# Moved waits, the value copy before the probability copy, and a new ending of the last phase, in a state-space plus local-attention kernel

## The reference

```python
for l in range(6):                                   # B=2, N=1024, D=128, 16 heads of 64
    q, k, v = split(x @ Wqkv[l])                     # 128 -> 3 x 1024
    q, k = rotary(l2norm(q) * qs, l2norm(k) * ks)
    p = softmax(8 * q @ k.T)                         # windows of 32 queries over 64 keys
    x = x + (p @ v) @ Wo[l]
    a, g = split(layernorm(x) @ W1[l] + b1)          # 128 -> 2 x 341
    x = x + (a * gelu(g)) @ W2[l] + b2
out = resid + gate * x
```

## Time and profile before

| | |
|---|---|
| time, median of 3 | 2083.33 us (2079.34 to 2084.64) |
| the profiled execution, its own time | 2082.23 us |
| its span, first to last instruction | 2080.4 us |
| PE busy | 1992.2 us (96%) |
| DVE busy | 1520.1 us (73%) |
| ACT busy | 1383.3 us (66%) |
| POOL busy | 1227.6 us (59%) |
| granted PE clock, mean | 0.975 of full speed |

### The profile page before, as it was taken

The page is one execution under the profiler, slowest core; times in us unless marked ns, Lnnn a source line. Parts: engine busy times, 40 slices in busy tenths (PEclk is TensorE's granted clock), DMA queues, the critical chain, the costliest instruction groups (busy, mean ns, idle before and its releaser), DMA issues. The chain is left out here.

```text
span 2080.4 us, 82225 instructions
## 1 busy us (share of the span) xinstructions
PE 1992.2 (96%) x32996; PEld 1395.7 (67%) x32996; DVE 1520.1 (73%) x2879; ACT 1383.3 (66%) x4165; POOL 1227.6 (59%) x1376
## 2 busy tenths in 40 slices
PE   7788798999999999999999999999999999999987
PEld 3333233887687786876877868768768677687672
DVE  1499896886786776867867768679678687686763
ACT  4532233886786776867867777678678776686772
POOL 1376774775585564855756756559456566575550
PEclk9888888999999999999999999999999999999998
DMA  1421110311131111221111211112211111121110
GB/s 62 134 71 71 60 61 4 102 44 39 38 93 40 38 44 32 50 84 37 47 36 40 87 37 45 38 35 57 79 38 47 38 41 40 32 54 30 27 29 21
DMA packets 148091, 104.30 MB, mean 50 GB/s; under 512 B 15778, under 2 KB 140256, under 8 KB 146176
## 3 DMA queue, kind: packets, MB, share of 16 engines
q1 hardware_dynamic: 147712, 99.07, 17.1%
HBM read 48.31 MB, written 1.18 MB: 24 GB/s over the span
## 5 line engine op out<-in xcount | busy, mean ns | idle before, releaser
L1401 POOL TENSOR_TENSOR QK<-QK,RN 128x512 f32<-128x512 f32 x384 | 400.2, 1042 | 375.2 <-ACT RN L1134 360.1
L1144 ACT ACTIVATE PR<-ps,MN 128x64 f32<-128x64 f32 x1536 | 355.9, 315 | 155.6 <-DVE MN L1262 140.0
L1009 PE MATMUL ps<-W,XS 128*128 128x256 f32 x1536 | 434.9, 406 | 5.1 <-PEq L64 4.1
L1396 POOL TENSOR_TENSOR QK<-PC,PS 128x256 f32<-128x256 f32 x384 | 279.7, 728 | 247.8 <-PE ps L995 243.8
L1170 ACT COPY QKT<-ps 128x512 f32<-128x512 f32 x384 | 224.6, 585 | 245.9 <-PE ps L995 245.8
L1286 DVE TENSOR_REDUCE SS<-SQ 128x8 f32<-128x512 f32 x384 | 262.2, 683 | 57.6 <-ACT SQ L1177 55.6
L1009 PEld LDWEIGHTS ps<-W,XS 128*128 128x128 f32 x1536 | 260.8, 189 | 61.6 <-issue 4.9
L1397 POOL TENSOR_TENSOR QK<-PC,PS 128x256 f32<-128x256 f32 x384 | 280.8, 731 | 0.0
L1262 DVE TENSOR_REDUCE MN<-ps 128x4 f32<-128x256 f32 x384 | 162.9, 424 | 149.8 <-PE ps L957 148.1
L1305 DVE TENSOR_TENSOR PC<-ps,TC 128x512 f32<-128x512 f32 x384 | 261.2, 680 | 0.1
L1307 DVE TENSOR_TENSOR PS<-ps,TS 128x512 f32<-128x512 f32 x384 | 260.4, 678 | 0.0
(11 more groups left out here) (137 smaller groups left out, 3216.3 us busy)
## 6 DMA issues: line engine op xcount, KB each, us to landing
V<-V SPq DMA_DIRECT2D x384, 97.5 KB, 2.2
scr<-B_rows SPq DMA_DIRECT2D x32, 512.0 KB, 3.6
V<-V SPq DMA_DIRECT2D x288, 32.5 KB, 2.4
W<-in_Wqkv SPq DMA_DIRECT2D x40, 192.0 KB, 2.9
TC<-in_tcos SPq DMA_DIRECT2D x6, 1024.0 KB, 5.1
TS<-in_tsin SPq DMA_DIRECT2D x6, 1024.0 KB, 8.5
WO<-in_Wo SPq DMA_DIRECT2D x6, 512.0 KB, 4.1
W<-in_W SPq DMA_DIRECT2D x6, 341.0 KB
```

Of the source, the lines that this page charges most:

```text
L1009: mm = nc.tensor.matmul(ps[:, par, k * 2 * P:(k + 1) * 2 * P], cols[k], W[:, i, 0:2, :].rearrange("p t m -> p (t m)"), start=True, stop=True)
L1144: e = nc.scalar.activation(PR[:, m % 2, h, slot * DH:(slot + 1) * DH], ps[:, 3 + h, slot * DH:(slot + 1) * DH], ACT.Exp, scale=-1.0, bias= ...
L1396: nc.gpsimd.tensor_tensor(QK[:, par, :, 0:hd], PC[:, par, :, 0:hd], PS[:, par, :, hd:DH], ALU.add)
L1401: nc.gpsimd.tensor_tensor(QK[:, par, :, :], QK[:, par, :, :], bcast_last(RN[:, m // 2 % 2, 8 * par:8 * par + 8], DH), ALU.mult).then_inc(q ...
```

## The change

There are four parts.

1. In steady steps the first value product loses its wait for `v_cp`, and the first projection product its wait for `prods`. The wait for `prods` goes to the first mask product. The wait for `pT` at the first score product stays.
2. ACT copies V before PT (in the feed-forward step too, between the GELUs).
3. Eight draining steps are left behind step 384. Ten of the sixteen output products of the last phase are issued inside them (`early_wo`), after the probability transposes of their step. The rest of the phase follows in code of its own, over six banks instead of one; DVE takes the layer norm's scaling from POOL.
4. The output is no longer formed by DVE and transposed. `out_rows` lets PE add `XRES.T` and `XT.T @ diag(gate)` in one bank, with two products of 128x128 for each 128 columns; POOL makes the two diagonal matrices DG at the start. Batch 0's rows are made in the ending before the feed-forward, batch 1's last.

```diff
@@ scores, values, project
+                    if steady(n) and h == 0:
+                        pe.wait_ge(prods, n - 1)
...
-                wait(pe, v_cp, min(n, NSTEPS))
+                    wait(pe, v_cp, min(n, NSTEPS))
...
-                wait(pe, prods, n - 1)
+                if not steady(n):
+                    wait(pe, prods, n - 1)
...
@@ places and banks
+        LAST = 2 * DEPTH - 1
+        DRAIN = NSTEPS + 8
+        early_wo = {1: [(0, 0), (0, 1)], 2: [(0, 2)], 3: [(0, 3)], 4: [(0, 4), (0, 5)], 5: [(0, 6)],
+                    6: [(0, 7), (1, 0), (1, 1)]}
...
+            return (7, 0, 3)[k % 3] if t == LAST else (2, 7)[k % 2]
...
@@ new functions on PE
+            def out_pair(t, c, k):
+                mm = nc.tensor.matmul(ps[:, wo_bank(t, c), :], WO[:, k, :], OT[:, c, k, :], start=(k == 0),
+                                      stop=(k == PAIRS - 1), skip_group_check=True)
...
+            def out_rows(b, c, bank):
+                for k in range(4):
+                    cols = slice((2 * b + c) * CH + k * P, (2 * b + c) * CH + (k + 1) * P)
+                    nc.tensor.matmul(ps[:, bank, k * P:(k + 1) * P], XRES[:, cols], ident[:], start=True, stop=False)
+                    mm = nc.tensor.matmul(ps[:, bank, k * P:(k + 1) * P], XT[:, cols], DG[:, b, :], start=False, stop=True)
...
+                if n == NSTEPS + 1:
+                    pe.wait_ge(prods, NSTEPS)
+                for c, k in early_wo.get(n - NSTEPS, ()):
+                    pe.wait_ge(oT, PHASE * LAST + 4 * k + 2 + 2 * c)
+                    out_pair(LAST, c, k)
...
@@ ACT
                     copy_out(n)
                     squares(n)
+                    copy_v(n)
                     copy_p(n)
-                    copy_v(n)
...
+            deviation(LAST, 0)
+            inverse(LAST, 0)
+            copy_rows(0)
+            copy_rows(1)
+            deviation(LAST, 1)
+            inverse(LAST, 1)
+            load_set(nc, act, GELU)
+            gates(LAST, range(6))
+            copy_rows(2)
+            copy_rows(3)
...
@@ DVE
+            for c in range(2):
+                add_attn(LAST, c)
+                centre(LAST, c)
+                dve.wait_ge(fsq, 2 * LAST + c + 1)
+                last_norm(c)
+            hidden(LAST)
+            add_ffn(LAST)
```

More of the change, by code:

```diff
@@ L864, in _ @@
             sp.wait_ge(s_v0, 1)
-            for n in range(NSTEPS + PHASE):
-                u, t = n % PHASE, n // PHASE - 1
+            for n in range(DRAIN):
+                u, t = n % PHASE, n // PHASE - 1 if n < NSTEPS else -1
                 if n < NSTEPS:
@@ L1081, in feed_forward @@
                         pe.wait_ge(hid, 6 * t + k - 1)
-                    nc.tensor.matmul(ps[0:size, banks[k % 2], :], W1[:, m0:m0 + size], CEN[:, c, :],
-                                     start=True, stop=True).then_inc(up_ps, 1)
+                    up_product(t, k)
                 if t % 2 == 0:
@@ L1087, in feed_forward @@
                     pe.wait_ge(hid, 6 * t + 5 + c)
[L1088 to L1094, removed]
+                    w2_product(t, c)
+            def out_rows(b, c, bank):
[3 more added lines that the diff above has]
+                    mm = nc.tensor.matmul(ps[:, bank, k * P:(k + 1) * P], XT[:, cols], DG[:, b, :], start=False, stop=True)
+                mm.then_inc(fT_ps, 1)
+            for n in range(DRAIN):
+                u, t = n % PHASE, n // PHASE - 1 if n < NSTEPS else -1
                 if u == U_FFN + 1 and t >= 0:
@@ L1218, in gates @@
                     wait(act, w2_ps, 2 * t)
-                    nc.scalar.activation(HID[0:size, c, m, :], ps[0:size, banks[k % 2], :], ACT.Gelu,
+                    nc.scalar.activation(HID[0:size, c, m, :], ps[0:size, gate_bank(t, k), :], ACT.Gelu,
                                          bias=vec(6 + m, t // 2, size)).then_inc(gel, 1)
-            for n in range(NSTEPS + PHASE):
-                u, t = n % PHASE, n // PHASE - 1
+            for n in range(DRAIN):
+                u, t = n % PHASE, n // PHASE - 1 if n < NSTEPS else -1
                 norm_pair(n)
@@ L1249, in _, with copy_rows @@
                             inverse(t, c)
[L1250 removed]
+            def copy_rows(c):
                 act.wait_ge(fT_ps, c + 1)
[L1252 removed]
+                nc.scalar.copy(OUT[:, 4 * c:4 * c + 4, :].rearrange("p k m -> p (k m)"), ps[:, 3 + c, :]).then_inc(fcp, 1)
+            deviation(LAST, 0)
[8 more added lines that the diff above has]
+            copy_rows(3)
         @block.vector
@@ L1374, in _ @@
             nc.gpsimd.memset(lnb[:], float(np.log(LN_SCALE) / 2)).then_inc(s_lnb, 1)
+            for b in range(B):
+                nc.gpsimd.tensor_scalar(DG[:, b, :], ident[:], MOD[:, 5, b:b + 1], None, ALU.mult).then_inc(s_dg, 1)
             def scale_rows(l):
```

162 lines of the change are left out of this document (110 added, 52 removed).

## The result

The changed kernel takes 2100.12 us (median of 3 runs, 2095.63 to 2100.2), against 2083.33 us. The ratio is 1.0078, with a 95% interval of 1.0048 to 1.0107: slower, by more than the bound that the prediction set for a case of its own (0.3%), where it had forecast 2080 us and held 2088 us for the upper end. The profiled execution took 2095.63 us, its span is 2093.8 us (2080.4 before).

The account below looks back on a forecast made before the run. PE was taken as busy throughout regular stretches, with ACT's ring of copies next at 0.01 us. +7.4 + 2.7 + 0 - 13.5 = -3.4 us gave 2079.9 us from 2083.33, forecast as 2080, range 2072.5 to 2088.

Parts of the forecast that it names:

- Part 1, the waits that go: Waits dropped at PE's first value and projection products: already over, the gap comes of the shape change, so worth 0.
- Part 2, V ahead of PT: ACT's copy order: PT still released 0.01 us ahead of the score load, so regular steps give 0 to -3 us.
- the eleven places: Places, one per phase, where PT is already last to come and its 0.26 us delay counts nearly in full: +2.7 us.
- rival C: V can't start before 1304.03, so PT is 0.03 to 0.04 us late every regular step: 2089 to 2092; chance 0.12.
- Part 1, the wait that is added: First mask product waits for `prods` behind POOL's table scalings: 20 of 40 places at 0.37 us, +7.4 us, at most +14.8.
- Parts 3 and 4, the ending: Output products moved into the drain and a reworked ending: saves 13.5 us, between 10 and 17.
- the walk: Piece-by-piece timing of the new ending, from chunk 0's projection done at 2028.7 to the end at 2066.6, saving 13.8.
- Four products enter this ring: In the drain, four output products at 0.89 us delay the chain of transposes, scores, values and DVE's ON: +3.5 us.
- about 2 us stick: Of the three output products behind those four in the drain, about 2 us remain as cost.
- A: Removed waits did cost something, ACT's ring gives its 0.01 us and the ending saves 16: -8.9 us, 2074.4; chance 0.30.
- the ring: ACT's chain from score products through exponents, squares and copies back to scores: leaves 0.01 us, at most -3 us in all.
- B: Every table scaling pays its 0.37 us at the mask, 14.8 in all: +4.0 us, 2087.3; chance 0.15.

Follow-up runs that it names:

- Run 3: The kernel before with V copied ahead of PT and the first value product's wait for `v_cp` removed in steady steps: 2111.76 us, ratio 1.0147.
- run 2: The kernel before with only the order of ACT's copies changed, V ahead of PT: 2107.56 us, ratio 1.0138.
- run 5: The kernel before with V copied ahead of PT, and SP also waiting for PT's copy before it issues V's two shifts: 2100.02 us, ratio 1.0076.
- run 4: The kernel before with only the wait for `prods` moved to the first mask product in steady steps: 2093.4 us, ratio 1.0052.
- run 7: The kernel before with the `prods` wait moved to the mask and DVE's clamp replaced by a bias in ACT's logarithm: 2084.3 us, ratio 0.9998.
- run 1: The changed kernel with parts 1 and 2 taken back, so the new ending alone: 2064.1 us, ratio 0.9917 to the kernel before.

## Why the prediction was wrong

**The sign.** It was made of -13.5 for the ending and +10.1 for the rest. In the profiled executions, cut at the last full step, these are -15.2 and +30.3; another -1.6 lies ahead of the first scores, a stretch that lasts 371.4 to 377.8 us in the kernels here though no edit is aimed at it. The gain came about nearly as forecast; the loss was three times the forecast one.

**Part 1, the waits that go: right.** Run 3 beside run 2 differs by 0.2 us in the steady part. The gap at the change of shape stayed: from the last value product's start to the projection's load are 0.145 us in the median before and after. The Trainium skill's rule that a change of the tiling mode empties the engine ("TensorEngine Tiling (Array Packing)", section Key Properties), which the prediction cites, spoke for the same, and the trace agrees with it by this 0.145.

**Part 2, V ahead of PT: the step that failed.** "PT 1304.25, its end 1304.62, release 1304.67. The load stands at 1304.68. So a regular step costs 0, with 0.01 us to spare." The start was right. The end was put together from two rows that don't go together: the earliest start, 0.49 us behind the squares, from the earlier trace rows, and the duration 0.37 from the earlier trace rows, where PT starts at 0.53. In the earlier trace rows itself the copy that starts at 0.49 lasts 0.42, and so ends at 0.91 behind the squares, as the one of the earlier trace rows does (0.53 + 0.37 = 0.90). The whole trace of before says the same: 54 such copies start 0.49 us behind the squares and last 0.41 in the median, 248 start at 0.53 and last 0.37, and both kinds end at 0.90. A copy that starts early here doesn't end early. With V's end at 0.90 as now and PT's some 0.27 behind it, as V's end stood behind PT's in the earlier trace rows (1304.67 - 1304.40), the release comes 1.22 us behind the squares against 1.18 of before: 0.04 us late, in 300 to 330 steps +12 to +13, and with the 2.7 for the eleven places +15. The prediction had 0 to -3 for the regular steps; run 5 measured +15.1 in all. This is rival C's price and place (0.03 to 0.04 us, +9 to +12), though C had another cause, V's start; I gave it 0.12 on a slack of one hundredth, and the two rows that decided it were both in front of me.

**What the prediction lacked.** V's copy releases SP too. V ahead of PT moves the issue of the two shifts from the score load to 0.29 us ahead of it, and then the value products are stretched in 153 of 377 steps: 25.9 - 15.1 = 10.8 us (runs 2 and 5). I had followed V's copy to PE only, and not to SP, which waits for the same signal. Which of the two DMAs does it, and by what, is open: in the step shown above their data moves only from 1389.4 on, behind the last value product, and in 103 of the 153 stretched steps of run 2 no DMA packet at all is under way while the value products start. No run separates the two.

**Part 1, the wait that is added: right in mechanism, and nearly in size.** Alone it costs +8.3 us (run 4) against +7.4, with 32 shorter waits in place of 20, and run 7 shows that it is the clamp that POOL holds. What wasn't seen is that this depends on where DVE stands against POOL. In the regular step before, the clamp started ahead of POOL's second addition by 0.02 us:

```profile
1306.16 0.17 DVE L1293 TENSOR_SCALAR SS<-SS 128x16 f32<-128x16 f32 x1
...
1306.18 0.74 POOL L1397 TENSOR_TENSOR QK<-PC,PS 128x256 f32<-128x256 f32 x1
```

A late PT shifts the two, and the clamp is held in regular steps as well: in run 2, where only the order of the copies is changed, 141 clamps last over 0.25 us, against 78 before and 142 in the changed kernel. This makes the clamp worth 12.5 us in the changed kernel.

**Parts 3 and 4, the ending: right in mechanism and in size.** The profiled executions give -15.2 us, and run 1 -15.3, against -13.5 within 10 to 17. The bare ending behind the last scores is 18.1 shorter, but that leaves out the four products ahead of them. To compare the walk, both times are taken from the last full step: its scores stand at 1999.11 in run 1 and at 2002.46 before, 3.35 us later. The prediction has chunk 0's projection done at 2028.7. Run 1 has it done at 2024.74, where the add starts, so at 2028.1 on the scale of before. "Four products enter this ring: +3.5 us" measured +2.8 (14.6 to 17.4 us from the last full step's scores to the last scores), and "about 2 us stick" 1.8, from the last scores to the end of the last value products. The rest came 0.9 us sooner than predicted: from that add to the next 8.8 us (9.3 predicted for chunk 1's products), the table load 17.2 us behind the add (predicted 2046.8 - 2028.7 = 18.1), and from the load's end to the span's 2061.7 - 2043.2 = 18.5 (2066.6 - 2048.1 = 18.5). With 0.6 for chunk 0 that makes the predicted 13.8 into 15.3. The low clock that bounded it from the other side didn't come: it was 0.99 to 1.00 over the new ending.

**The chances.** A (faster, 0.30) rested on a gain of the ring, which there is not; B was too dear for the moved wait alone, as 32 waits and not 40 times 0.37 were paid. C had the place and the price of the late PT, but its 2089 to 2092 us lack the stretch and the clamps held in regular steps. The forecast and its range held no case in which two of the terms are off together.

## What to carry to other kernels

A copy's end comes from its own row: take start and duration from the same row, or take the end alone, measured from the end of what stands ahead of it. Where a slack of 0.01 us is multiplied by 300 steps, the term is not zero but plus or minus the error of the two rows, and the slower bound belongs into the sum. When an instruction is moved, list all that wait for its signal, the DMA queue too; and where DVE's clamp is ahead of POOL's operation by 0.02 us, a small shift can turn the order round.

## What the runs showed of the hardware

- Value products of 64x32 pieces lost up to 0.1 us, mostly in front of the last one, in 153 of 377 steps when SP had issued the first shift of V 0.3 us ahead of the first score load, and in 14 when it was issued with it (runs 2 and 5). In 103 of the 153 no DMA packet was under way.
- A small operation on DVE (128x16) lasted 0.17 us, and 0.43 and 0.64 where an operation of POOL was under way. All 142 that took over 0.25 us in the changed kernel ended within 0.05 us of the end of an operation of POOL.
- Behind the squares, a copy of 128x256 that started 0.49 us later took 0.41 us in the median (54 times), and one that started 0.53 later 0.37 (248 times): both ended at 0.90.
- The new ending, with PE busy for 39.8 of 45.0 us, was granted 1.00 of the clock; the last 58.4 us of before, with PE busy for 43.0, had 0.86.
- From the last 64x32 value product's start to the load for a 128x128 product were 0.145 us, before and after.
